# Five changes of order around a pipelined two-layer graph attention kernel: half-row counts, interleaved stacking transfers, loop hints, and three moved steps

## The reference

```
h = relu(layernorm(x))                                   # layer 0
Q, K, V = h Wq^T + bq, h Wk^T + bk, h Wv^T + bv          # 8 heads of 32
attn = softmax(where(adj == 0, -inf, Q K^T / sqrt(32)))
x = x + (attn V) Wo^T + bo

h = relu(layernorm(x))                                   # layer 1
e_k = leaky_relu((h * a_k) h^T, 0.2)      for k = 0..3
scores = e_k where adj == k + 1, else -9e15
x = x + softmax(scores) h
```

## Time and profile before

| what | value |
|---|---|
| median of 3 runs | 3785.14 us (3775.22 to 3788.88) |
| time of the profiled execution | 3785.14 us |
| its span, first to last instruction | 3783.3 us |
| PE busy | 3454.1 us, 91% of the span |
| DVE busy | 2850.7 us, 75% |
| ACT busy | 2464.4 us, 65% |
| POOL busy | 1125.2 us, 30% |
| chain that ended last | PE 61%, issue 11%, ACT 10%, SPq 7%, DVE 7% |
| mean granted PE clock | 0.974 |

### The profile page before, as it was taken

The page is one execution under the profiler, slowest core; times in us unless marked ns, Lnnn a source line. Parts: engine busy times, 40 slices in busy tenths (PEclk is TensorE's granted clock), DMA queues, the critical chain, the costliest instruction groups (busy, mean ns, idle before and its releaser), DMA issues.

```text
span 3783.3 us, 97534 instructions
## 1 busy us (share of the span) xinstructions
PE 3454.1 (91%) x34096; PEld 2916.1 (77%) x34096; DVE 2850.7 (75%) x5622; ACT 2464.4 (65%) x4548; POOL 1125.2 (30%) x568
## 2 busy tenths in 40 slices
PE   5889999899998999999899998999989999998975
PEld 4678778787787878778787787877878787787864
DVE  4777778787787878878777787878778787887752
ACT  4775767657676676766757676666766757676541
POOL 2232423323232232423323232232422324233212
PEclk8999999999999999999999999999999999999988
DMA  4141412314132141412414132141321414123101
GB/s 120 51 113 54 128 36 81 93 58 122 40 103 72 59 121 55 112 53 67 107 54 128 40 100 75 54 125 49 110 57 56 122 54 128 40 86 89 37 27 44
DMA packets 166740, 294.99 MB, mean 78 GB/s; under 512 B 25536, under 2 KB 75968, under 8 KB 166080
## 3 DMA queue, kind: packets, MB, share of 16 engines
q1 hardware_dynamic: 166080, 286.63, 27.0%
HBM read 169.09 MB, written 16.78 MB: 49 GB/s over the span
## 4 chain that ended last, share of the span: by engine, by line
PE 61%; issue 11%; ACT 10%; SPq 7%; DVE 7%; DMA 2%; POOL 0%; DVEq 0%; ACTq 0%; POOLq 0%
PE pT L1082 15%; PE pG L1017 13%; PE pG L1095 11%; PE pG L1152 8%; PE ps L1070 7%; SPq L250 6%; ACT sm L490 4%; PE pT L1143 3%; PE pG L1051 3%; DMA adj_half<-in_adj_dram 2%; ACT pt L501 2%; DVE sm L754 1%; DVE pt L766 1%; PE pG L1108 1%; ACT sm L546 1%
## 5 line engine op out<-in xcount | busy, mean ns | idle before, releaser
L754 DVE CUSTOM_DVE_ANT_0 sm<-ps,bias 128x1024 f32<-128x1024 f32 x1024 | 1244.1, 1215 | 20.6 <-issue 17.0
L1082 PE MATMUL pT<-ident,sm 128*128 128x128 f32 x8192 | 1099.7, 276 | 127.0 <-ACT pt L501 108.9
L1082 PEld LDWEIGHTS pT<-ident,sm 128*128 128x128 f32 x8192 | 946.5, 141 | 345.0 <-ACT sm L490 140.4
L490 ACT ACTIVATE sm<-sm,mn 128x1024 f32<-128x1024 f32 x1024 | 1180.5, 1153 | 48.5 <-DVE mn L754 48.0
L501 ACT COPY pt<-pT 128x512 f32<-128x512 f32 x1024 | 596.3, 582 | 592.6 <-PE pT L1082 592.4
L766 DVE COPY pt<-pT 128x512 f32<-128x512 f32 x1024 | 703.0, 687 | 287.1 <-PE pT L1082 281.4
L417 POOL TENSOR_SCALAR gbias<-adj_half 128x512 bf16<-128x512 int32 x256 | 505.2, 1973 | 1324.3 <-DVE mn L865 1030.1
L1070 PE MATMUL ps<-ks,qs 96*128 96x512 f32 x2048 | 760.9, 453 | 76.7 <-DVE mn L754 64.1
L400 POOL TENSOR_SCALAR bias<-adj_half 128x512 bf16<-128x512 int32 x256 | 492.5, 1924 | 785.5 <-DMA adj_half<-in_adj_dram 712.0
L1095 PE MATMUL pG<-pt,v 128*32 128x128 f32 x16384 | 530.7, 283 | 27.5 <-DVE x L889 18.5
L1095 PEld LDWEIGHTS pG<-pt,v 128*32 128x32 f32 x16384 | 455.1, 114 | 87.9 <-issue 39.3
(11 more groups left out here) (104 smaller groups left out, 3328.1 us busy)
## 6 DMA issues: line engine op xcount, KB each, us to landing
adj_half<-in_adj_dram SPq DMA_DIRECT2D x512, 256.0 KB, 2.9
ks<-parts SPq DMA_DIRECT2D x384, 128.0 KB, 2.4
qs<-parts SPq DMA_DIRECT2D x384, 128.0 KB, 2.6
x<-in_x_dram SPq DMA_DIRECT2D x16, 1024.0 KB, 5.6
out_dram<-x SPq DMA_DIRECT2D x128, 128.0 KB, 2.6
x<-in_x_dram SPq DMA_DIRECT2D x32, 256.0 KB, 3.5
rb<-in_x_dram SPq DMA_DIRECT2D x16, 256.0 KB, 3.2
sq<-in_x_dram SPq DMA_DIRECT2D x16, 256.0 KB, 3.3
```

The source lines that it names most:

```text
L490: nc.scalar.activation(sm[:, ring(t), :], sm[:, ring(t), :], ACT.Exp, scale=-1.0, bias=mn[:, t:t + 1], accum_out=den[:, t:t + 1]).then_inc ...
L754: nc.vector.tensor_tensor_reduce(out=sm[:, ring(t), :], in0=ps[t % 2][:, :], in1=bias[:, node, :], scale=1.0, scalar=3e38, op0=ALU.add, op ...
L1082: last = nc.tensor.transpose(pT[c][:, j * P:(j + 1) * P], sm[:, ring(t), m * P:(m + 1) * P], ident[:, :])
```

## The change

Five things change; the arithmetic stays what it was.

1. `most_kind` counts each half of 512 columns by an instruction of its own, with a count of its own (`most` has two columns for each block, `LOADS` = 16 counts for each graph). `load_adj` waits for the count of its own half only. Each of ACT's counts waits for the one before it.
2. `first_stacks` no longer stacks K of four heads and then Q of four heads. Its first call stacks K and Q of heads 0 and 1 and waits for products 1 and 3; its second call stacks heads 2 and 3.
3. The five loops are written with the plain `Fori`, without the hint of the back edge.
4. ACT: `edge_exp` moves from slot 3 of a period to the end of slot 2; in slot 45 `edge_copy` of block 7 comes behind `exp`; `layer_norm` moves from slots 5, 6 and 7 (ahead of the copies) to slots 7 and 8 (behind them, four instructions each).
5. DVE: `edge_leaky` comes right behind the second `edge_mask`, one `mask` earlier; `result` of block 7 comes ahead of the `mask` in slot 46; `front_low` of piece 1 moves from slot 45 to slot 46; `layer_aggregate` moves behind the V read-outs of slot 4 and `layer_shift` to slot 6.

```diff
-PROMPT = (4, 45)
-NORM = {5: (0, 1, 2, 3), 6: (4, 5), 7: (6, 7)}
...
-        most = sb("most", [P, NT], F)
+        most = sb("most", [P, 2 * NT], F)
...
                     if made is not None:
-                        sp.wait_ge(most_made, made)
+                        sp.wait_ge(most_made, made + c - 1)
...
-            def first_stacks(f, q):
-
-                sp.wait_ge(qk_h, 8 * f + 2 * q + 2)
-                settle(sp)
-                sp.wait_ge(qk_l, 8 * f + 2 * q + 2)
-                settle(sp)
-                for head in range(HG):
-                    stack(head, q)
+            def first_stacks(f, n):
+
+                if n == 0:
+                    for q in range(2):
+                        sp.wait_ge(qk_h, 8 * f + 2 * q + 2)
+                        settle(sp)
+                        sp.wait_ge(qk_l, 8 * f + 2 * q + 2)
+                        settle(sp)
+                        stack(0, q)
+                    stack(1, 0)
+                    stack(1, 1)
+                else:
+                    stack(2, 0)
+                    stack(3, 0)
+                    stack(2, 1)
+                    stack(3, 1)
...
-            with nc.Fori(1, B - 1, engines=bass.OrderedEngineSet([sp.engine]), hint_back_edge=True) as b:
+            with sp.Fori(1, B - 1) as b:
                 stage(b, True)
...
-            def most_kind(f, node, loaded, free=None):
+            def most_kind(f, node, loaded, free=None, first=False):
 
                 for c in range(2):
                     act.wait_ge(adj_in[c], 16 * (loaded + 1))
-                if free is not None:
-                    act.wait_ge(l_masked, free)
-                if node:
-                    act.wait_ge(most_made, NT * f + node)
-                nc.scalar.activation(gbias[:, :], adj_half[:, :, :].rearrange("p c n -> p (c n)"), ACT.Square,
-                                     bias=mhalf[:, 0:1], scale=1.0,
-                                     accum_out=most[:, node:node + 1]).then_inc(most_made, 1)
+                    if free is not None:
+                        act.wait_ge(l_masked, free)
+                    if not first:
+                        act.wait_ge(most_made, LOADS * f + 2 * node + c - 1)
+                    nc.scalar.activation(gbias[:, c * HALF:(c + 1) * HALF], adj_half[:, c, :], ACT.Square,
+                                         bias=mhalf[:, 0:1], scale=1.0,
+                                         accum_out=most[:, 2 * node + c:2 * node + c + 1]).then_inc(most_made, 1)
...
                 for s in range(TILES):
-                    if earlier and s == EDGE + 4 * NT:
-                        edge_copy(o, NT - 1)
                     if s + 1 < TILES:
                         exp(b, s + 1)
                     elif later:
                         exp(b + 1, 0)
-                    if earlier and EDGE + 3 <= s < EDGE + 3 + 4 * NT and (s - EDGE) % 4 == 3:
-                        edge_exp(o, (s - EDGE - 3) // 4)
-                    if earlier and EDGE + 4 <= s < EDGE + 4 * NT and (s - EDGE) % 4 == 0:
+                    if earlier and EDGE + 4 <= s < EDGE + 4 + 4 * NT and (s - EDGE) % 4 == 0:
                         edge_copy(o, (s - EDGE - 4) // 4)
-                    if earlier and s in NORM:
-                        layer_norm(o, NORM[s])
                     copy(b, s, not earlier)
...
+                    if earlier and EDGE + 2 <= s < EDGE + 2 + 4 * NT and (s - EDGE) % 4 == 2:
+                        edge_exp(o, (s - EDGE - 2) // 4)
...
+                    if earlier and s in (7, 8):
+                        layer_norm(o, range(4 * (s - 7), 4 * (s - 7) + 4))
...
+                    if earlier and s == EDGE + 1 + 4 * NT:
+                        result(o, NT - 1, pG[bank("sum", NT - 1)])
                     if s + 2 < TILES:
                         mask(b, s + 2, not earlier, made)
                     elif later:
                         mask(b + 1, s + 2 - TILES, False, base + NT)
-                    if earlier and s == EDGE + 1 + 4 * NT:
-                        result(o, NT - 1, pG[bank("sum", NT - 1)])
-                    if earlier and EDGE + 2 <= s < EDGE + 2 + 4 * NT and (s - EDGE) % 4 == 2:
-                        edge_leaky(o, (s - EDGE - 2) // 4)
...
-                    for kind, n in ahead[s - 1] + behind[s - 1] if s and s - 1 not in PROMPT else ():
+                    for kind, n in ahead[s - 1] + behind[s - 1] if s and s != 5 else ():
                         if kind != "edge":
                             evacuate(kind, n)
-                    if earlier and s == 4:
-                        layer_aggregate(o)
...
                     for kind, n in behind[s]:
                         if kind == "edge":
                             evacuate(kind, n)
-                    for kind, n in ahead[s] + behind[s] if s in PROMPT else ():
+                            edge_leaky(o, n // 2)
+                    for kind, n in behind[s] if s == 4 else ():
                         evacuate(kind, n)
...
                     if earlier and s == 4:
+                        layer_aggregate(o)
+                    if earlier and s == 6:
                         layer_shift(o)
```

More of the change, by code:

```diff
@@ L243, in mask_adj @@
                     settle(sp)
-                load_adj(f, node, base + NT + node, NT * f + node if node else None)
+                load_adj(f, node, base + NT + node, LOADS * f + 2 * node if node else None)
             def stack(head, q):
@@ L280, in front_load @@
                 load_xf(b + 1, 2)
-                sp.wait_ge(most_made, NT * (b + 1))
+                sp.wait_ge(most_made, LOADS * (b + 1))
                 settle(sp)
@@ L293, in stage @@
                 second_stacks(b, 0)
-                load_adj(b, NT - 1, base - 1, NT * b + NT - 1)
+                load_adj(b, NT - 1, base - 1, LOADS * b + 2 * (NT - 1))
                 second_stacks(b, 1)
-                sp.wait_ge(most_made, NT * (b + 1))
+                sp.wait_ge(most_made, LOADS * (b + 1))
                 settle(sp)
@@ L344, in _ @@
                 sp.dma_start(adj_half[:, c, :], adj_t[0, 0][:, c * HALF:(c + 1) * HALF]).then_inc(adj_in[c], 16)
-            sp.wait_ge(most_made, 1)
+            sp.wait_ge(most_made, 2)
             settle(sp)
@@ L351, in _ @@
             for t in range(2, NT):
-                sp.wait_ge(most_made, t)
+                sp.wait_ge(most_made, 2 * t)
                 settle(sp)
@@ L363, in _ @@
                     load_x1(0)
-                sp.wait_ge(most_made, NT + t)
+                sp.wait_ge(most_made, LOADS + 2 * t)
                 settle(sp)
@@ L442, in stage @@
                         front_rstd(b + 1)
-                    edge_bias(o, t, base + t, NT * (b + 1))
+                    edge_bias(o, t, base + t, LOADS * (b + 1))
                 if later:
@@ L461, in _ @@
                 masks(1, node, NT + node)
-            with nc.Fori(1, B - 1, engines=bass.OrderedEngineSet([pool.engine]), hint_back_edge=True) as b:
+            with pool.Fori(1, B - 1) as b:
                 stage(b, True)
@@ L467, in _ @@
             for t in range(NT):
-                edge_bias(B - 1, t, base + t, NT * B)
+                edge_bias(B - 1, t, base + t, LOADS * B)
         @block.scalar
@@ L625, in _ @@
                 front_high(0, n, n % 2)
-            most_kind(0, 0, 0)
+            most_kind(0, 0, 0, None, True)
             for n in range(8):
@@ L636, in _ @@
             stage(0, False, True)
-            with nc.Fori(1, B - 1, engines=bass.OrderedEngineSet([act.engine]), hint_back_edge=True) as b:
+            with act.Fori(1, B - 1) as b:
                 stage(b, True, True)
@@ L789, in flag_rows @@
             def flag_rows(b):
[L790 removed]
+                dve.wait_ge(most_made, LOADS * (b + 1))
                 nc.vector.tensor_reduce(most_all[:, :], most[:, :], AX, ALU.max).then_inc(flag_most, 1)
                 dve.wait_ge(flag_most, b + 1)
[L793 removed]
+                nc.vector.tensor_scalar(flagf[:, :], most_all[:, :], HALF / 4 + 0.5, None, ALU.is_gt).then_inc(flag_f, 1)
             def flag_cell(b, i):
@@ L978, in _ @@
             stage(0, False, True)
-            with nc.Fori(1, B - 1, engines=bass.OrderedEngineSet([dve.engine]), hint_back_edge=True) as b:
+            with dve.Fori(1, B - 1) as b:
                 stage(b, True, True)
@@ L1269, in _ @@
             stage(0, False, True)
-            with nc.Fori(1, B - 1, engines=bass.OrderedEngineSet([pe.engine]), hint_back_edge=True) as b:
+            with pe.Fori(1, B - 1) as b:
                 stage(b, True, True)
```

2 lines of the change are left out of this document (removed).

## The result

| | before | after |
|---|---|---|
| median of the runs, us | 3787.0 (3775.2 to 3799.6, 4 runs) | 3963.7 (3956.3 to 3968.7, 4 runs) |
| ratio, 95% interval | | 1.0465 (1.0426 to 1.0502) |
| profiled execution, us; span | 3785.1; 3783.3 | 3959.6; 3957.6 |
| mean granted TensorE clock | 0.974 | 0.958 |

The change costs 177 us. The forecast was 110 us more (3895), its range ended at 3960. The sign is right, the size is not, and the time lies 4 us above the range.

What follows compares the result with a forecast made beforehand. PE's work was taken to bound most of a stage, elsewhere PE's back edge, SP's issuing and loads, or DVE and ACT. 7.4 us times 14 looped stages, 104, plus 4 and 2, made 110 on 3785.14: 3895 us, range 3825 to 3960.

Steps and rivals of the forecast that it cites:

- Edge leaky: Behind the second edge_mask: delays one mask 1.4 us; costs 0.3 us a stage over seven periods, 0.35 in slot 16.
- Loop hints: At the back edges: four engines get stalls, PE has its 3.7 us already; 0, bounds -0.1 and 1.0 us an edge.
- Rival C: At the back edge: PE's hint itself makes its branch long, so removal saves 64 us over 13 edges; chance 0.06.
- Slots 45 to 47: PE waits for ACT's later edge copy and the read-out comes late: 2.0 us in each of 14 looped stages.
- Stacks: SP's queue: nine transfers behind a product wait delay adjacency loads 3.5 us; net 2.9 us in stages 0 to 14.
- Half counts: ACT's adjacency counts: two halves take slightly longer, felt in slot 61; 0.35 us a stage, bounds -0.3 and 1.0.
- Layer norm: Slots 5 to 12: four instructions move from ACT's waiting into a dense stretch; 0.5 us a stage, bounds 0 and 1.5.
- Clock: More waiting in slots 16 and 55 to 60 gives slow-clock stretches; 1.0 us a looped stage, bounds 0 and 3.

Runs made afterwards that it cites:

- leaky_apart: Kernel before with edge_leaky behind the second edge_mask, and GpSimd writing the second half of gbias only after the leaky step; ratio 1.0008.
- stacks_counts: Kernel before with the changed order of SP's transfers for the stacks and the halved adjacency counts on ACT together; ratio 1.0140.
- late_only: Kernel before with only the slots 45 to 47 edits: edge copy behind exp, DVE's result ahead of the mask, front 1 read out later; ratio 0.9961.

## Why the prediction was wrong

Two steps failed. Edge leaky was mis-sized, and by the sections it holds most of what the sum missed. Loop hints had the mechanism wrong.

**Loop hints: "PE has its 3.7 us already, hint or not ... I take 0".** The earlier trace rows showed a median of 3.70 us and I read it as every branch. Two of 13 were short. The hint's worth is 3.5 us for each branch it serves, and how many it serves depends on the rest of the kernel: 0 to 11 of 13. Inside the changed kernel the hints are worth 59 us against 0 (bound 1.0 us an edge, 13 us). Rival C had a part of the truth, that PE's stall can go and that this gives over 3.5 us and the clock, with the wrong cause: the hint does not make the stall, it removes it. Of the 177 us this step holds little, since the kernel before had only two short branches to lose: PE's 13 branches take 53.5 us in place of 43.0, and slots 61 to 4 show 1.26 us a stage. The 59 us are what the hints would save once the other edits are in, and they are no part of the sum by sections. How much the other edits cost depends on it: with all hints in both kernels they cost 113 us (3904 against 3791), of which ten short branches have already repaid a part, without any 164 us (3964 against 3800). That my sum of 110 is near the first is luck: what the leaky step costs more is hidden there by the branches that came out short.

**Edge leaky is the mis-sized term**: 0.3 + 0.35 forecast, 3.96 us a stage measured in those slots (1.88 + 2.08); the difference, 3.3 us times 14, is 46 us of the 67 that were missed. Two things were wrong. In slots 17 to 43 the queue's order costs what I said (0.24 us in leaky_apart), but the leaky step now starts together with POOL's write, and both get longer. I counted 1.4 us between the two masks. Alone it is 1.33 us (leaky_apart, 1241.54 to 1242.87), beside POOL 1.74 (1257.44 to 1259.18). The cover was just gone by my own numbers (1243.6 against 1243.72), so the 0.41 us more show at once. In slot 15 the whole 1.39 us of the queue shows (2.29 to 3.68 us), where I let a wait take most.

The Trainium skill ("SBUF — State Buffer", Who interferes with whom) says that VectorE and GpSimd share a port pair, and that a VectorE instruction with two SBUF inputs contends for it with a GpSimd instruction that reads SBUF. The summary of the same page in the Trainium skill adds that the second one to issue "fully blocks" until the first has finished. L877 has two SBUF inputs, POOL's reads `adj_half`: POOL's 2.93 - 1.92 = 1.01 us is near L877's 1.22. The trace agrees that far. It does not agree on L880: blocked for POOL's whole instruction it would have ended behind 1260.56, and it lost 0.42 us. Nor does it where POOL is first: in the kernel before POOL's instruction started at 1241.25 and took its usual 1.92 us, and the leaky instruction at 1242.20 took its usual 1.22 us. Why they lengthen each other in one order and not in the other stays open.

**Slots 45 to 47**: 2.0 forecast, bounds 1.0 and 2.5. Alone 2.38, in the whole 2.46 us in slots 44 to 51. The mechanism is right and the term short by 0.4. Most of the rest of the 3.01 us there belongs to the half counts (0.27 + 0.18).

**Stacks**: 2.9 with bounds 2.0 and 3.5. 3.36 us alone in slots 48 to 63, by the nine transfers as told. In the whole it is worth 5.2 us (73 us by the stages over 14), in part because the new order also cancels what the halved counts give. I had counted the halves' gain inside the 2.9; stacks_counts shows that it isn't there. And ACT waits one load earlier than I had it (2.49 us at block 4).

**Half counts**: 0.35 forecast. With the old order they are a gain: -1.44 us a stage by the profile, 0.4 of it PE's shorter branches, and -0.8 by the runs, below the bound of -0.3. **Layer norm**: 0.5 against 0.24, right.

**Clock**: 1.0 a looped stage. The trace knows two levels of the granted clock, 1.0 and 0.5. So the share of the span at the lower level is twice what the mean lacks to 1: 197 us before, 332 after. Of these 135 us more, each costs PE at most half, by this estimate 4.8 us a stage. No experiment separates this from the waits that bring it on; it is part of each section's cost above.

**What stays open.** The list of DMA transfers shows instruction blocks of 16384 bytes, all on one queue; I take them for PE's. In the eleven profiles with PE's hint, all 43 short branches had a block 2.2 to 3.4 us ahead of them, and all 100 long ones had their last block at least 6.8 us ahead and the next 0.6 to 2.6 us behind the branch's start. In the seven without PE's hint all 91 were long, 46 of them with a block 2.3 to 3.5 us ahead. That fits a late block which is the hinted one, but the list does not say what a block holds, so it is not shown. The hint itself (BRANCH_PREFETCH_HINT) stands at the start of each stage, in the kernel before at 237.1 us for the branch at 461.3. What decides whether it helps was not found; PE's program in late_only is that of before, so it is not PE's own instructions.

## What to carry to other kernels

List the branches of a loop one by one; a median hides a stall that comes and goes, and an edit that does not touch the loop's branch can switch it (late_only). When single edits don't sum to the whole, look for a resource that each one alone was paid from: here waits in slots 55 to 60 and PE's short branches. When two engines are released by the same event, ask what they do beside each other: one wait that kept GpSimd off VectorE's step gave back 51 us.

## What the runs showed of the hardware

- A hinted back edge of PE took 0.46 to 0.65 us or 3.2 to 5.0 us; both occur in one execution (0 to 11 of 13 short over eleven kernels). Without a hint it took 3.4 to 5.7 us, 91 of 91 times.
- ACT's and DVE's branch records read 0.04 to 0.09 us with and without a hint. Without one, ACT stands idle for 1.4 to 3.5 us and DVE for 2.5 to 3.6 us soon behind it (78 edges in six kernels); with one it is 0 on ACT and at most 0.41 us on DVE (156 edges).
- A 128x512 int32 instruction of POOL started 0.07 us behind a 128x1024 VectorE instruction with both inputs in SBUF takes 2.93 in place of 1.92 us, and the one-column VectorE instruction behind that 0.57 in place of 0.15 (92 of 128 periods in the changed kernel, none with the two kept apart).
- The same POOL instruction started 0.95 us ahead of it (1241.25 against 1242.20 in the kernel before) lengthens neither.
- Two counts of 512 columns take 1.42 us on ACT (from 1421.33 to the next instruction's start at 1422.75), where one of 1024 took 1.15.
